# Attention of a Mamba, attention and mixture-of-experts layer: the causal steps of all head groups run first, then all context steps

## What is computed

```python
q, k, v = _heads(x @ Wq + bq), _heads(x @ Wk + bk), _heads(x @ Wv + bv)
att = jnp.einsum('bhqd,bhkd->bhqk', q, k) * scale
att = jnp.where(causal[None, None], att, -jnp.inf)
y = jnp.einsum('bhqk,bhkd->bhqd', jax.nn.softmax(att, axis=-1), v)
qc = _heads(x @ Wcq + bcq)
kc, vc = _heads(cross_input @ Wck + bck), _heads(cross_input @ Wcv + bcv)
attc = jnp.einsum('bhqd,bhkd->bhqk', qc, kc) * scale
y = y + jnp.einsum('bhqk,bhkd->bhqd', jax.nn.softmax(attc, axis=-1), vc)
return y.transpose(0, 2, 1, 3).reshape(x.shape[0], T, C) @ Wp + bp
```

## Time and profile before

| | us |
|---|---|
| median of 3 runs | 1846.45 |
| range of the runs | 1843.0 to 1854.02 |
| the profiled execution | 1853.68 |
| its span, first to last instruction | 1851.9 |
| exponentials L1809, busy, 768 in the span | 361.6 |
| maxima of context jobs L1837, busy, 256 in the span | 297.8 |
| maxima of causal jobs L1841, busy, 256 in the span | 107.3 |

### The profile page before, as it was taken

How to read it: one execution, slowest core, us unless ns; L and a number is a source line. 1 busy time by engine, 2 the same in 40 slices (tenths; PEclk the granted TensorE clock), 3 DMA queues, 4 the chain that set the end, 5 groups by cost and what they waited for, 6 DMA issues and landing times. The chain is left out here.

```text
span 1851.9 us, 19445 instructions
## 1 busy us (share of the span) xinstructions
PE 1474.7 (80%) x6520; PEld 730.4 (39%) x6520; DVE 1306.0 (71%) x2025; ACT 818.5 (44%) x1586; POOL 660.6 (36%) x634
## 2 busy tenths in 40 slices
PE   5597889984987799875878899846677998779995
PEld 2353422242554232342544222422232322468884
DVE  6998488748996788379994887479976782533324
ACT  3543336745543266654433377443333566212221
POOL 2565341212864312117653422128643222112220
PEclk9799979996999899987999799969998899689998
DMA  4940452003002531021004520030014221147744
GB/s 132 340 134 1 111 126 56 23 3 127 18 1 54 142 77 34 13 92 53 1 0 119 118 56 25 1 118 21 0 43 128 64 48 63 53 147 253 230 160 137
DMA packets 128069, 153.87 MB, mean 83 GB/s; under 512 B 19110, under 2 KB 107695, under 8 KB 125921
## 3 DMA queue, kind: packets, MB, share of 16 engines
q1 hardware_dynamic: 124224, 143.96, 26.7%
q0 software_dynamic: 3744, 8.66, 1.3%
HBM read 102.82 MB, written 50.99 MB: 83 GB/s over the span
## 5 line engine op out<-in xcount | busy, mean ns | idle before, releaser
L170 PE MATMUL PS<-arena 128*32 128x512 f32 (+10 forms) x4150 | 830.2, 449 | 84.4 <-DVE maxs L1837 22.0
L170 PEld LDWEIGHTS PS<-arena 128*32 128x32 f32 (+3 forms) x4150 | 363.3, 128 | 524.4 <-ACT arena L1809 205.4
L1809 ACT ACTIVATE arena<-PS 128x512 f32<-128x512 f32 (+3 forms) x768 | 361.6, 549 | 225.5 <-PE PS L170 224.4
L1391 POOL TENSOR_TENSOR arena<-arena 128x1024 f32<-128x1024 f32 x128 | 305.0, 2384 | 238.7 <-DVE arena L1417 140.0
L1837 DVE TENSOR_REDUCE maxs<-PS 128x1 f32<-128x1024 f32 x256 | 297.8, 1214 | 41.5 <-PE PS L170 41.2
L1417 DVE TENSOR_TENSOR_SCAN arena<-PS,arena 128x1024 f32<-128x1024 f32 x128 | 292.1, 2282 | 6.1 <-ACT PS L1366 6.1
L1366 ACT ACTIVATE PS<-arena,A_neg 128x511 f32<-128x511 f32 x256 | 165.9, 681 | 240.8 <-DVE arena L1417 191.5
L170 PE MATMUL PS<-arena,ident 128*128 128x512 f32 (+1 forms) x560 | 259.6, 590 | 5.4 <-DVE arena L1426 5.4
L1426 DVE TENSOR_TENSOR arena<-arena,PS 128x1024 f32<-128x1024 f32 x128 | 156.3, 1221 | 6.9 <-PE PS L170 2.8
L1553 POOL TENSOR_SCALAR_AFFINE_SELECT arena<-arena 128x128 f32<-128x128 f32 x256 | 72.6, 294 | 234.2 <-ACT arena L1809 230.3
L170 PE MATMUL PS<-bc,bc_sel 96*128 96x512 bf16 x128 | 52.3, 409 | 121.3 <-DVE arena L1426 115.0
(11 more groups left out here) (263 smaller groups left out, 1548.1 us busy)
## 6 DMA issues: line engine op xcount, KB each, us to landing
arena<-in_ew SPq DMA_DIRECT2D x46, 512.0 KB
arena<-stack_parts SPq DMA_DIRECT2D x288, 64.0 KB, 2.3
rows_in<-nil SPq DMA_DIRECT2D x16, 1088.0 KB, 12.5
arena<-b_rows SPq DMA_DIRECT2D x16, 1024.0 KB, 8.0
stack_parts<-arena SPq DMA_DIRECT2D x40, 384.0 KB, 2.6
arena<-stack_parts SPq DMA_DIRECT2D x96, 128.0 KB, 4.2
arena<-rows_in SPq DMA_DIRECT2D x23, 272.0 KB, 4.7
xn<-dens SPq DMA_DIRECT2D x24, 256.0 KB
```

The lines of the kernel that those rows point to most:

```text
L170: return nc.tensor.matmul(o, l, r, start=start, stop=stop)
L1391: nc.gpsimd.tensor_tensor(b_sb[i % 2], u[:, 2 * kh:2 * kh + 2, :], Brow[:, n, :].unsqueeze(1).to_broadcast([P, 2, T]), ALU.mult).then_inc( ...
L1809: nc.scalar.activation(probs[(HG * s + h) % NPR][:, 0:N], ring_bank(n)[:, 0:N], ACT.Exp, scale=HD ** -0.5).then_inc(S["ring_read"], 1)
```

## The change

The steps are put in another order: the 16 causal steps of groups 0 to 3 come first, then the 32 context steps. The maximum jobs follow: those of group 0 and half of group 1 before the steps (with four context jobs of group 0 between them, as before), then the causal jobs of groups 1 to 3, the rest of group 0's context jobs, and those of groups 1 to 3; `JOBS_AT` gives two a step, three in steps 3, 4, 9 and 10, none in the last ten. All four Q and K stacks stay resident; C and KC keep three. The causal values accumulate in banks 6 and 7 in turn, so the causal scores have a ring of two banks (4, 5), and bank 7 joins when the last causal copy is out (step 17). The causal sums of all groups are inverted and spread together; the context sums group by group. In `entry`, the last group's causal side is already done, so half of the turning and spreading is left.

```diff
+            def ring_bank(n):
+                return bank((4, 5)[n % 2] if n < PAIRED else (4, 5, 7)[(n - PAIRED) % 3])
+
+            def step(s):
+                return (s // TT, CAUSAL, s % TT) if s < NG * TT else \
+                    ((s - NG * TT) // CS, CONTEXT, (s - NG * TT) % CS)
...
+            JOBS_AT = [2, 2, 2, 3, 3, 2, 2, 2, 2, 3, 3] + [2] * (NSTEP - 11)
...
+                def context_sums(g):
+                    sp.wait_ge(S["pv_copied"], NG + g + 1)
+                    sp.dma_start(den_c[0:HG * TT, :], YX[g % 2][HD:P:32, :]).then_inc(S["dens_out"], 16)
+                    sp.wait_ge(S["den_ready"], g + 2)
...
+                load_max_rows(1, CAUSAL)
+                load_heads(3, 0)
+                load_heads(3, 1)
+                all_stored(sp)
+                load_heads(1, 2)
+                load_heads(1, 3)
                 if b + 1 < NB:
                     sp.dma_start(x_sb[:], x_in[b + 1].rearrange("(t p) n -> p t n", p=P)).then_inc(x_loaded, 16)
                     sp.wait_ge(S["v_mm"], 3 * TT)
                     sp.dma_start(ctxT[:], ctx_t[b + 1]).then_inc(ctx_loaded, 16)
+                load_max_rows(2, CAUSAL)
+                load_max_rows(3, CAUSAL)
                 load_max_rows(0, CONTEXT)
...
+                causal_sums_in(2)
+                causal_sums_in(3)
+                sp.wait_ge(S["pv_mm"], NG * TT + CS)
+                load_heads(3, 2)
+                load_heads(3, 3)
+                context_sums(0)
+                load_max_rows(2, CONTEXT)
+                context_sums(1)
+                load_max_rows(3, CONTEXT)
+                context_sums(2)
...
+                for s in range(NSTEP):
+                    g, side, k = step(s)
+                    if s in ONES:
+                        pe.wait_ge(S["ones_ready"], ONES[s])
+                    if k == 0:
+                        pe.wait_ge(max_rows[g], 16 * 3 * (side + 1))
+                    pending = turned[0] < len(TURNS) and J > last_job(*TURNS[turned[0]])
+                    jobs = list(range(J, min(J + JOBS_AT[s], len(JOBS))))
+                    J += len(jobs)
+                    scores(s, (0, 1))
+                    if pending:
+                        max_rows_out(*TURNS[turned[0]])
+                    elif jobs:
+                        max_job(jobs[0])
+                    scores(s, (2, 3))
+                    if jobs and not pending:
+                        max_job(jobs[1])
+                    if s:
+                        values(s - 1)
+                    for j in jobs if pending else jobs[2:]:
+                        max_job(j)
...
+                for g, side in TURNS[2:]:
+                    end = last_job(g, side) + 1
+                    if (g, side) == (1, CONTEXT):
+                        maxima(range(at, at + 8))
+                        invert_causal()
+                        at += 8
+                    if side == CONTEXT and g >= 2:
+                        maxima(range(at, at + 8))
+                        invert_context(g - 2)
+                        at += 8
+                    maxima(range(at, end))
+                    at = end
+                    negated_parts(g, side)
+                invert_context(NG - 2)
```

More of the change, by code:

```diff
@@ L308, in decoder @@
         stack_in = [sem(f"stack_in{g}_{kind}") for g in range(2) for kind in ("causal", "context")]
-        max_rows = [[sem(f"max_rows{g}_{side}") for side in ("causal", "context")] for g in range(NG)]
+        max_rows = [sem(f"max_rows{g}") for g in range(NG)]
         weights_in = [sem(f"weights_in{i}") for i in range(3)]
@@ L361, in decoder @@
         yt_end = used[0]
-        YS = [(ar(T), ar(T)) for _ in range(2)]
+        YX = [ar(T) for _ in range(2)]
+        Q.append(q_last[:])
+        K.append(stack(T))
         assert used[0] <= pre_at
@@ L757, in decoder @@
         CS = 2 * TT
[L758 removed]
         KJOBS = HG * 2
[L760 to L763 removed]
+        CJOBS = HG * TT
+        NSTEP = NG * (TT + CS)
         def scatter(pool, k):
@@ new lines, in sync @@
+                sp.wait_ge(S["pv_copied"], NG)
+                for g in range(NG):
+                    sp.dma_start(den_c[g * HG * TT:(g + 1) * HG * TT, :], YT[g][HD:P:32, :]).then_inc(S["dens_out"], 16)
+                load_heads(2, 2)
+                load_heads(2, 3)
+                sp.wait_ge(S["den_ready"], 1)
+                sp.dma_start(causal_dens.rearrange("g h (q p) -> (g h q) p", p=P), den_c[:]).then_inc(S["dens_kept"], 16)
+                sp.wait_ge(S["dens_kept"], 16)
+                causal_sums_in(0)
@@ L1543, in low, with ones_rows, ones_done @@
                         .then_inc(S["parts_ready"], 1)
[L1545 to L1554 removed]
+                made = [0]
+                def ones_rows(stack):
+                    nc.gpsimd.memset(stack[SK:SR], 1.0).then_inc(S["ones_ready"], 1)
+                    made[0] += 1
+                def ones_done():
+                    pool.wait_ge(S["ones_ready"], made[0])
                 link = chain(pool, S["pool_chain4"])
@@ L1649, in max_rows_out @@
                 def max_rows_out(g, side):
[L1650 to L1659 removed]
+                    assert turned[0] == turn_of(g, side)
@@ new lines, in max_rows_out, with scores @@
+                    pe.wait_ge(S["max_done"], last_job(g, side) + 1)
+                    nc.tensor.transpose(bank(0)[0:HG * TT, 0:P], maxs[:, turned[0] % 2 if side else 2 + g % 2, :],
+                                        ident[:]).then_inc(S["mt_mm"], 1)
+                    turned[0] += 1
+                def scores(s, heads):
+                    g, side, k = step(s)
+                    for h in heads:
+                        n = HG * s + h
+                        if n == PAIRED + 2:
+                            pe.wait_ge(S["pv_copied"], NG)
+                        elif n >= PAIRED + 3:
+                            pe.wait_ge(S["ring_read"], n - 2)
+                        elif n >= 2:
+                            pe.wait_ge(S["ring_read"], n - 1)
@@ L1686, in values @@
+                        if side == CONTEXT:
+                            last = mm(bank(6)[rows], VC[:, k, HG * g + h, :], p, k == 0, k == CS - 1)
+                        else:
+                            last = mm(bank(6 + g % 2)[rows, k * P:T], V[:, k, HG * g + h, :], p[:, 0:T - k * P],
+                                      k == 0, k == TT - 1)
                     last.then_inc(S["pv_mm"], 1)
```

411 lines of the change are left out of this document (177 added, 234 removed).

## The result

| | before | after |
|---|---|---|
| median | 1845.25 us (4 executions, 1843.0 to 1854.02) | 1911.83 us (4 executions, 1904.95 to 1916.05) |
| profiled execution | 1853.68 | 1904.95 |
| mean granted clock in it | 0.911 | 0.907 |

The ratio is 1.0342, interval 1.0316 to 1.0368: slower, by 66.6 us between the medians, and by 51.3 between the two profiled executions. The forecast was 1867 with a range up to 1887, so the sign was right and the size was not. One of the six executions of the last experiment took 2923.37 us; it is in the median given there (1910.36 without it) and not in the ratio.

The account below looks back on a forecast made before the run. The prediction took TensorE to bound the regular context step. It summed +8.4 us in each of three sequences, +4.4 in the fourth and -8.7 at the ends to +20.9 on the median 1846.45: 1867, range 1826 to 1887.

Parts of the forecast that it names:

- A: Step 8: TensorE waits for group 2's causal maxima rows, queued behind loads up to `ctxT`; 6.3 us, last sequence 3.3.
- A's clock: Behind the wait at step 8: TensorE runs at 1.2 GHz for a while, costing 1.9 us, last sequence 0.9.
- B: First context sums, queued behind 12 head loads: VectorE stands 7.4 us, TensorE 7.0, slow clock 3; 10.0 a sequence.
- the ring: Causal steps with two score banks: up to 0.5 us in the long steps, taken as already inside the step figures.
- The 27.3: Steps 8 to 16: 25.4 us of work, with 12 context jobs in a row on VectorE, plus 1.9 of slow clock.
- turns: Context stretch: 1.0 us each for two turns, 0.3 for the last, which has no jobs; 2.3 together.
- the causal inversion: Context stretch: the inversion comes when its sums have barely landed and costs 0.8 us.
- Its ones rows (one more K stack) end before the first mask: nothing: GpSimd ahead of the steps: filling one more K stack's ones rows costs nothing, 1 if not.
- the start gains 0.7: Ahead of the steps: two more projections fill TensorE's 4.17 us wait for heads, against four more causal jobs; 0.7 gained.
- The end of a sequence: Half the turning and spreading passes go: 1.9 us saved, 3.0 in the last sequence, 8.7 together.
- Small DMAs pass the bulk: Rival at both waits: small DMAs land ahead of the queued loads, giving 1830 us; chance 0.13.
- More waits: Rival: group 1's context rows land late at step 24 and slow clock reaches steps 0 to 3; 1880 to 1885, chance 0.12.

Follow-up runs that it names:

- the last experiment: Changed kernel with the read-backs of the causal sums of groups 2 and 3 issued behind the write of the first context sums: 1911.24 us, ratio 1.0341.
- the two-bank run: Kernel before the change with its ring of score banks cut from three (4, 5, 7) to two (4, 5): 1917.95 us, ratio 1.0359.
- the kernel with A alone removed: Changed kernel with group 2's causal maxima rows issued ahead of the loads of C and KC of group 1, `x_sb` and `ctxT`: 1883.88 us, ratio 1.0194.
- the one without A and B: Changed kernel with group 2's causal maxima rows and group 0's context sums both issued ahead of the loads: 1840.07 us, ratio 0.9977.
- The one with three edits: Changed kernel with both moves in SP's order, and GpSimd's ones rows for K of groups 1 and 2 filled behind the fifth tile: 1829.99 us, ratio 0.9885.
- the run without B: Changed kernel with group 0's context sums issued ahead of the 12 loads of C and KC of group 3: 1874.82 us, ratio 1.0148.

## Why the prediction was off

Right: the place, the cause and nearly the price of both waits; that nothing of the context stretch gives them back; that the change is slower. What failed are terms that were set small or at nothing, and the base. The working was 1874.6 for the profiled execution; it came out at 1904.95, 30.4 more. The table splits the difference, all four sequences together; what stands ahead of and behind the steps is the rest of the two spans.

| stretch | predicted | measured | difference |
|---|---|---|---|
| steps 0 to 8, with A | 3 x 28.1 + 25.1 = 109.4 | 119.0 | +9.6 |
| steps 8 to 16, with A's clock | 3 x 27.3 + 26.3 = 108.2 | 115.7 | +7.5 |
| steps 16 to 47, with B | 4 x 98.8 = 395.2 | 401.7 | +6.5 |
| ahead of and behind the steps | -8.7 - 4 x 0.7 = -11.5 | -4.5 | +7.0 |

**Steps 0 to 8: the ring.** The step that failed is "is inside these figures". The 10.3 for four causal steps came from a kernel with three banks, and the two-bank run shows 11.2 for the same piece. The sum also counts three jobs more than before in these eight steps; `JOBS_AT` has two. With both put right it is 2 x 11.2 + 2 x 0.4 = 23.2; the kernel with A alone removed and the one without A and B have 23.0 to 24.3. (The one with three edits has 23.7, 23.4, 25.7 and 26.0; in the last two the granted clock is 0.50 for 3.4 us shortly before step 8.) The mechanism had been named, the fourth score waits for the second exponential; the row to read it from did not exist, and zero was taken where 0.5 a step was the upper end.

**A itself.** Predicted 6.3, and 30.4 - 23.7 = 6.7 in the first sequence. The rows land at 29.6 for the 27.8 of the sum: SP starts its loads at 9.7 after step 0 and not at 8.8, since the steps ahead of group 1's turn are slower and its rows take 2.41 to issue for 1.77; and the rows land 0.6 behind `ctxT` and not with it. SP was late and TensorE was late by as much, so the stand came out right, which is luck. With the clock A was 3 x 8.2 + 4.2 = 28.8; the edit that takes it away saves 27. Small DMAs did not pass the bulk, 6.3 us for 1.7. The Trainium skill's page "DMA: Bandwidth & Descriptors", section "Queues, rings and completion order", says that each ring is consumed in order, though completion is not FIFO per issuing engine. By the first, a load with pieces on all 16 rings would hold back what is queued behind it; the landings here agree, the rows 0.6 behind `ctxT`.

**Steps 8 to 16: the clock, and a sum that was right twice with two wrong terms.** The 27.3 holds in sequences 1 and 2 (27.3 both times). But without A and B the same stretch takes 27.4, 26.4, 27.8 and 26.4, where the sum had 25.4. The two of 26.4 run at 2.4 GHz throughout, so the work itself was 1.0 too small (the ring fits, no run separates it here); the other two have 3.4 us at 1.2 GHz in step 10. Against the 26.4, A's clock was 0.9 in sequences 1 and 2, for 1.9 in the sum, and 4.1 in 3 and 4, for 1.9 and 0.9: there the half clock lasts as long as the windows of 19.5 and 17 us. The prediction took its length from one place of before. How long the low clock stays is not fixed by the wait, and it isn't A's alone: the run without wait A has a stay of 17 us and 31.9 for these steps. The Trainium skill's page "TensorE: Matmul & The Clock Gate", section "HAM oscillation — how this bites in real kernels", tells that TensorE falls to the low clock while it waits for a DMA and begins the next piece of work there; the rows behind A and B agree, but neither it nor a run here tells why two sequences of four recover so late.

**Steps 16 to 47: turns, not B.** B was set at 10.0, and steps 24 to 28 without it are 10.2 shorter. Its parts were wrong against each other. The sums were issued 8.05 after step 24 began (8.5), but were usable 7.5 later instead of 5.2, and VectorE stood 9.73 for 7.4. Of the 7.5 the two broadcasts are 2.9: with them moved it is 4.6, and VectorE stands 7.24. TensorE stood 8.43 for 7.0, and of the 10.8 that the first sequence loses against the run without B some 2.3 are left for the low clock, for 3 in the sum. The 6.5 comes from the turns. Steps 16 to 47 of the kernel without A and B have 90.2, 89.9, 90.4 and 90.3, all at 2.4 GHz, for the 88.8 of the sum. There the first context turn costs 1.9 to 2.7 over steps of 2.89, the second 1.4 and the last 0.3 to 0.7, where the sum has 1.0, 1.0 and 0.3; the causal inversion costs 0.3 for 0.8. In the first of them, 0.5 to 1.3 us is TensorE's wait at step 24.

**Ahead of the steps.** Two terms. "Its ones rows (one more K stack) end before the first mask: nothing": there are two more stacks at this place, and the first mask is not the next thing in GpSimd's order, the low parts of the tiles are. It cost 3.9, 4.3 and 3.1 in the three later sequences. This was the step with the clearest mistake: a count and an order that the code has in plain sight. And "the start gains 0.7": from first maximum to first exponential it is 2.0, 2.0 and 0.5 more; the fill of the 4.17 by more projections did not show. Together 16 us ahead of the steps of sequences 2 to 4, where -2.1 stood, and 0.2 in the first, where -0.7 stood.

**The end of a sequence.** TensorE after, behind the last step of sequence 1, answers to the earlier trace rows:

```profile
398.70 1.02 PE L172 MATMUL PS<-den_sel,arena 128*128 128x4 f32 x8 [0.87 <-ACT arena L1837]
...
401.53 1.46 PE L172 MATMUL PS<-xT,in_w 128*128 128x512 f32 x3
```

401.53 - 394.64 = 6.9; before, the same reading gives 9.0. It is 2.1 less, for 1.9 predicted. In the next two sequences before has 10.2 and 10.5, after 6.9 again, so the three ends give 9.1 for 5.7. The last sequence ends 3.5 sooner, for 3.0.

**The stretches that the change leaves alone.** In the profile of before, the stretch from the first matmul of the next block to the first scan takes 45.8, 48.9 and 48.6, in that of after 45.7 three times, with the same instructions. A window of it close ahead of the scan, in before and then in after:

```profile
819.80:826.60 6.80, 6.80 (x14) 3.93 (x13) 4.50 (x8) 6.67 (x11) 0.00 (x0) 0.50 0.84 354
```

```profile
846.50:853.30 6.80, 4.32 (x17) 2.88 (x16) 5.77 (x17) 6.69 (x11) 0.00 (x0) 1.00 0.96 398
```

TensorE works at 1.2 GHz in the one and at 2.4 in the other. That is 6.1; with 1.7 behind one scan before lost 7.8 in its profile which after did not. So the 7.0 of the table is, to 0.1, the 18.8 more ahead of the steps, less 3.4 and 0.5 at the ends, less this 7.8. How much of it is the luck of one execution isn't settled. In the nine other traces of the new order this stretch takes 48.5 in 9 of 27 cases, so the new order is not free of it. But the two-bank run, in the old order, has 45.8, 48.8 and 48.9 like before, and ends of 10.3, 11.6 and 11.6, where the new order has 6.9 in 29 of 30.

**The base.** Before's profile lies 8.4 above its median, after's 6.9 below. The sum of the terms is 20.9 (20.7 unrounded, and before's four sequences are 0.5 longer than four times the first); with the 30.6 of the table it gives the 50.8 between the two spans. The two times differ by 51.3, and the 15.3 lead to the 66.6 of the medians. Where in the other executions the 15.3 lie, no trace shows. The forecast was rightly put on the median and not on the one execution, but two profiles that lie on different sides of their medians can differ by a quarter of what is looked for.

**The rivals.** "Small DMAs pass the bulk" is refuted at both places. "Neither", 1798, is what the two edits should have given; 1840 came, for the terms above. "More waits" held in part: the context rows of group 1 do land behind two broadcasts just as step 24 begins, at the price of the smaller wait there; that the granted clock is 0.50 for the first 2 to 3 us behind step 0 is true of before too (2 to 6). The range ended at 1887 since it took only the bounds of A and B, and nothing for terms set at nothing.

## What to carry over

An engine's queue is read with every instruction that stands behind the moved one, up to the first on which another engine waits: the ones rows were checked against the masks, and eight low parts stood between. A duration read from a stage with other buffers (three banks for two) was too small, 10.3 for 11.2, and costs kept "inside the figures" belong in the range. When a wait goes, ask who else waits for the same answer: a late inversion freed VectorE and stopped SP.

## What the runs showed of the hardware

Three DMAs of 4 KB issued by SP behind 24 head loads and two of 512 KB landed after 6.3 us, 1.7 without anything ahead; 8 KB behind 12 head loads were usable after 7.5 us, 4.6 when 512 KB of broadcasts were not ahead of the loads, 2.95 with the broadcasts ahead and the loads behind it. Here the loads, not the broadcasts, were the larger part.

TensorE's clock came back at very different times behind the same wait. ScalarE's row for step 8 of the third sequence is

```profile
1079.79 1.08 ACT L1847 ACTIVATE arena<-PS 128x512 f32<-128x512 f32 x2 [7.53 <-PE PS L172]
```

for 7.60 in the first. There the granted clock was 1.00 by 272, less than 6 us behind the wait; here it is 0.50 up to 1095, 15 us behind it, with TensorE busy 15.31 of the 19.5. A stay of 17 us also came where no wait for a DMA stood ahead of it, in the run without wait A. The same instructions between attention and scan took 45.8 or 48.9 us in one execution, with a granted clock of 1.00 or 0.50 in the windows shown. So an edit that takes a local 2 us away, as the one on the broadcasts, can be seen in the trace and not in the time.
